# Attention layer with low-rank experts: the q, k and v projections made of split F32R operands

## The reference

```
qkv_in = rat_read(hidden, ...)          # three groups of 512 features per token:
    x = res.reshape(b, l, 512, 4)
    y = einsum('blhc,hoc->bloh', x, W)  # o = 0, 1, 2: q, k, v
    yn = (y - mean) * rsqrt(var + eps) * gamma + beta
q = einsum('bli,oi->blo', q_in, qkv_w[0])   # 512 x 512, the same for k and v
q, k = rope(q, pos), rope(k, pos)           # 16 heads of 32
scores = q k^T / sqrt(32), causal; o = softmax(scores) v
hidden = rat_write(hidden, o, ...)
... a second rat_read, a gated product with the context, a second rat_write,
    then low-rank experts
```

## Time and profile before

| what | us |
|---|---|
| median of 3 runs (lowest to highest) | 1682.9 (1682.56 to 1685.71) |
| the profiled execution's own time | 1683.9 |
| its span | 1682.1 |
| TensorE busy in the span | 1571.4 |
| VectorE busy | 1132.0 |
| ScalarE busy | 906.1 |
| GpSimd busy | 340.0 |
| projections (start to the first score) | 270.2 |

### The profile page before, as it was taken

One profiled execution on the slowest core, in us unless ns is written; L12 is line 12 of the kernel. 1 busy time (PEld: TensorE's weight loads), 2 busy tenths in 40 slices (PEclk: granted clock), 3 DMA queues, 4 the chain that ended last, 5 costly groups with the idle time before them and its releaser, 6 DMA issues.

```text
span 1682.1 us, 24567 instructions
## 1 busy us (share of the span) xinstructions
PE 1571.4 (93%) x9238; PEld 1170.6 (70%) x9238; DVE 1132.0 (67%) x1758; ACT 906.1 (54%) x1672; POOL 340.0 (20%) x326
## 2 busy tenths in 40 slices
PE   7999999999999987699999999898999999999986
PEld 6565555666666655577898777697777788875654
DVE  7877754888888867644463774874675864546777
ACT  5334235888888864445543566553567634543443
POOL 1424534555434300110002010012000002000000
PEclk8999999999999998699999999999999999999998
DMA  9657567999987646267677665567675666655642
GB/s 358 221 196 304 182 170 236 282 284 279 269 224 198 188 173 200 108 206 231 207 234 226 228 233 194 187 228 227 225 244 193 202 214 209 226 194 179 222 181 100
DMA packets 129370, 364.29 MB, mean 217 GB/s; under 512 B 15954, under 2 KB 45266, under 8 KB 113892
## 3 DMA queue, kind: packets, MB, share of 16 engines
q1 hardware_dynamic: 128964, 362.59, 66.9%
q10 hardware_dynamic: 288, 0.13, 0.0%
HBM read 276.55 MB, written 86.11 MB: 216 GB/s over the span
## 4 chain that ended last, share of the span: by engine, by line
PE 75%; DVE 13%; ACT 6%; issue 3%; DMA 2%; POOL 1%; SPq 0%; DVEq 0%; ACTq 0%
PE ps L1626 20%; PE ps L1638 8%; PE ps L555 7%; PE ps L1048 5%; PE ps L1035 4%; PE ps L1071 4%; PE ps L1651 4%; PE ps L1569 3%; PE ps L1541 3%; PE ps L1596 3%; PE ps L1584 3%; PE ps L514 3%; ACT a_p L1150 3%; PE ps L1526 3%; PE ps L1556 1%
## 5 line engine op out<-in xcount | busy, mean ns | idle before, releaser
L1626 PE MATMUL ps<-m_y_split,m_win 128*128 128x512 f32 x1536 | 388.5, 407 | 8.0 <-issue 7.8
L1626 PEld LDWEIGHTS ps<-m_y_split,m_win 128*128 128x128 f32 x1536 | 287.1, 191 | 78.3 <-issue 14.0
L1092 DVE TENSOR_REDUCE a_negmax<-ps 128x1 f32<-128x640 f32 (+7 forms) x176 | 180.8, 1027 | 59.8 <-PE ps L1038 58.8
L1150 ACT ACTIVATE a_p<-ps,a_negmax 128x128 f32<-128x128 f32 (+7 forms) x256 | 188.7, 750 | 28.9 <-DVE a_negmax L1092 26.6
L1638 PE MATMUL ps<-m_wods,m_y_split 128*128 128x316 f32 x768 | 179.2, 321 | 0.9 <-DVE m_hT L1823 0.9
L1048 PE MATMUL ps<-ident,a_p 128*128 128x128 f32 x1152 | 157.5, 275 | 1.3 <-DVE a_pT L1105 1.2
L1861 ACT ACTIVATE m_turned<-ps 128x512 f32<-128x512 f32 x128 | 74.7, 595 | 135.1 <-PE ps L1526 124.1
L1035 PE MATMUL ps<-a_k,a_q 128*128 128x512 f32 (+3 forms) x384 | 124.1, 402 | 16.0 <-ACT a_p L1150 14.1
L1638 PEld LDWEIGHTS ps<-m_wods,m_y_split 128*128 128x128 f32 x768 | 127.7, 191 | 3.8 <-issue 2.4
L1048 PEld LDWEIGHTS ps<-ident,a_p 128*128 128x128 f32 x1152 | 123.7, 142 | 3.4 <-DVE a_pT L1105 1.9
L1823 DVE TENSOR_TENSOR m_hT<-m_raw,ps 128x512 f32<-128x512 f32 x64 | 43.8, 685 | 112.7 <-PE ps L1626 112.2
(11 more groups left out here) (217 smaller groups left out, 2939.1 us busy)
## 6 DMA issues: line engine op xcount, KB each, us to landing
m_win<-mlp_in_split SPq DMA_DIRECT2D x128, 512.0 KB, 4.0
m_wods<-mlp_out_split SPq DMA_DIRECT2D x96, 316.0 KB, 3.2
m_wod<-in_wod1T SPq DMA_DIRECT2D x64, 316.0 KB, 2.9
p_xT<-in_xT SPq DMA_DIRECT2D x16, 1024.0 KB, 8.9
p_x<-in_x SPq DMA_DIRECT2D x16, 1024.0 KB, 10.4
a_q<-qk_split SPq DMA_DIRECT2D x64, 256.0 KB, 7.1
a_k<-qk_split SPq DMA_DIRECT2D x128, 128.0 KB, 7.0
mlp_in_split<-a_w_two SPq DMA_DIRECT2D x32, 512.0 KB, 5.4
```

The costliest lines, as they stand in the source:

```text
L1092: V.tensor_reduce(negmax[:, n % 4, 0:len(units[n][3])], by_head(n, score_banks(n)), AX_X, ALU.max, negate=True).then_inc(max_ready, 1)
L1150: m = S.activation(dst[:, j, :], src[:, j, :], ACT.Exp, bias=negmax[:, n % 4, j:j + 1], accum_out=rsum[:, si % 2, q * 4 + hh:q * 4 + hh + 1])
L1626: m = nc.tensor.matmul(bank_of("m", blk, step), win[s][:, wl, ic, :], y[k], start=(ic == 0 and p3 == 0), stop=(ic == HCH - 1 and p3 == 2))
```

## The change

Each operand of the q, k and v products is split into an upper half, rounded to F32R, and a lower half, the rest. Each product of two float32 operands becomes three F32R products: upper by upper, upper data by lower weights, lower data by upper weights.

- TensorE: `qkv` issues 12 F32R matmuls per step instead of 4 float32 ones. The turns of v (k = 8 to 11) leave the group before step 0 and stand between steps 3 and 4, after the read at step 3.
- ScalarE: `turn(blk, w)` makes the upper half of every k and the whole copy of those that VectorE doesn't (8 of 12); v's four come at step 3 ahead of `round_rope`. `weights_upper` makes the upper halves of the weights: q's before the first turn, k's after it, v's at step 3 of block 0.
- VectorE: `turn` makes whole copies of k = 0, 1, 4, 5, each after ScalarE's upper half, and lower halves of k = 0, 1; lower halves of q's weights ahead of, and of k's weights behind, the first block's turn.
- GpSimd: `lower` makes ten lower halves: k = 2 to 7 at the end of a block, 8 to 11 at step 3 behind the rotation and ahead of `read_a`; in block 0 also those of v's weights there.
- Buffers: y data in two sets of upper and lower halves of four k each (`halves_of`, `halves_are_free`); three rotation buffers in which the halves are made in place (`RR`), instead of two and four for halves; one table buffer and one `p_v` instead of two; five y buffers instead of six; the angles share the rotation buffers' place.
- SP: a block's table is loaded at the end of the block before; `load_first_heads` moves from after block 2 to step 3 of block 3, behind `store_qk` of pair 1.

```diff
-        XR, YR = 2, 6
+        XR, YR, RR = 2, 5, 3
...
-        wq = sb("p_wqkv", [P, 3 * HCH, H])
+        whi = sb("p_wqkv_hi", [P, 3 * HCH, H], F32R)
+        wraw = sb("p_wqkv", [P, 3 * HCH, H])
+        place[0] = wraw_place
+        wlo = sb("p_wqkv_lo", [P, 3 * HCH, H], F32R)
...
         def turn1_before(blk, k):
-            return 6 * blk + k // 4
+            return 6 * blk + (0, 1, 3)[k // HCH]
         def qk_before(blk, n):
-            return 6 * blk + 3 + n // 4
+            return 6 * blk + (2, 4)[n // 4]
+        RAW_BY_DVE, LO_BY_DVE = (0, 1, 4, 5), (0, 1)
+        def halves_of(blk, k):
+            s = (3 * blk + k // HCH) % 2
+            return yh[s][:, k % HCH, :], yl[s][:, k % HCH, :], yT[s][:, k % HCH, :]
+        def halves_are_free(e, blk, w):
+            if w == 1:
+                e.wait_ge(v_mm, 4 * blk)
+            else:
+                e.wait_ge(qk_mm, 8 * blk + 2 * w)
...
             def qkv(blk):
                 for n in range(8):
+                    if n == 4:
+                        turn(blk, 2)
                     pe.wait_ge(emptied[b], qk_before(blk, n))
+                    pe.wait_ge(whi_ready, HCH * w + HCH)
                     if w:
-                        pe.wait_ge(wkv_loaded, 16)
+                        pe.wait_ge(wklo_ready, HCH)
+                    else:
+                        pe.wait_ge(tables_ready, WQ)
                     for ic in range(HCH):
                         k = w * HCH + ic
-                        pe.wait_ge(emptied[4 + k % 4], turn1_before(blk, k) + 1)
-                        m = nc.tensor.matmul(ps[:, b, :], wq[:, k, col:col + P], yT[:, k, :],
-                                             start=(ic == 0), stop=(ic == HCH - 1))
+                        upper_is_there(blk, k)
+                        for j, ww in enumerate((whi, wlo)):
+                            nc.tensor.matmul(ps[:, b, :], ww[:, k, col:col + P], halves_of(blk, k)[0],
+                                             start=(ic == 0 and j == 0), stop=False)
+                    for ic in range(HCH):
+                        k = w * HCH + ic
+                        lower_is_there(blk, k)
+                        m = nc.tensor.matmul(ps[:, b, :], whi[:, k, col:col + P], halves_of(blk, k)[1],
+                                             start=False, stop=(ic == HCH - 1))
...
         # project_dve, turn(blk)
+                def raw(k):
+                    dve.wait_ge(turn1_mm, 12 * blk + k + 1)
+                    halves_are_free(dve, blk, k // HCH)
+                    dve.wait_ge(y1hi_ready, 12 * blk + k + 1)
+                    V.tensor_scalar(halves_of(blk, k)[2], ps[:, b, :], gam1[:, k:k + 1], bet1[:, k:k + 1],
                                     ALU.mult, ALU.add).then_inc(emptied[b], 1)
+                def lower(k):
+                    dve.wait_ge(emptied[b], turn1_before(blk, k) + 1)
+                    V.tensor_tensor(ylo_, whole, yhi_.bitcast(F32), ALU.subtract).then_inc(y1lo_dve, 1)
+                raw(0); raw(1); lower(0); lower(1); raw(4); raw(5)
             def rope(blk, pair):
-                dve.wait_ge(lo_ready, 2 * u - 2)
+                dve.wait_ge(split_stored[s], rope_stored_before(u, s))
...
         # project_dve, once
-            V.tensor_scalar(wq[:, 0:HCH, :], wq[:, 0:HCH, :], float(1.0 / np.float32(np.sqrt(HD))), None,
-                            ALU.mult).then_inc(tables_ready, 1)
+            for k in range(HCH):
+                dve.wait_ge(whi_ready, k + 1)
+                m = V.scalar_tensor_tensor(out=wlo[:, k, :], in0=wraw[:, k, :], scalar=QSCALE,
+                                           in1=whi[:, k, :].bitcast(F32), op0=ALU.mult, op1=ALU.subtract)
+            m.then_inc(tables_ready, 1)
             turn(0)
+            for k in range(HCH, 2 * HCH):
+                dve.wait_ge(whi_ready, k + 1)
+                V.tensor_tensor(wlo[:, k, :], wraw[:, k, :], whi[:, k, :].bitcast(F32),
+                                ALU.subtract).then_inc(wklo_ready, 1)
...
         # project_act
+            def weights_upper(w):
+                for k in range(HCH * w, HCH * w + HCH):
+                    act.wait_ge(wkv_loaded if w else wq_loaded, 16)
+                    S.activation(whi[:, k, :], wraw[:, k, :], ACT.Copy,
+                                 scale=1.0 if w else QSCALE).then_inc(whi_ready, 1)
+            def turn(blk, w):
+                for k in range(HCH * w, HCH * w + HCH):
+                    act.wait_ge(turn1_mm, 12 * blk + k + 1)
+                    halves_are_free(act, blk, w)
+                    S.activation(yhi_, ps[:, b, :], ACT.Identity, bias=bet1[:, k:k + 1],
+                                 scale=gam1[:, k:k + 1]).then_inc(y1hi_ready, 1)
+                    if k not in RAW_BY_DVE:
+                        S.activation(whole, ps[:, b, :], ACT.Identity, bias=bet1[:, k:k + 1],
+                                     scale=gam1[:, k:k + 1]).then_inc(emptied[b], 1)
...
-            turn(0)
+            weights_upper(0)
+            for w in range(2):
+                turn(0, w)
+            weights_upper(1)
             for blk in range(NBLK):
                 for step in range(12):
+                    if step == 3:
+                        turn(blk, 2)
+                        if blk == 0:
+                            weights_upper(2)
                     if step < 8 and step % 2:
                         round_rope(blk, step // 2)
...
         # project_pool
+            def lower(blk, ks):
+                for k in ks:
+                    pool.wait_ge(emptied[4 + k % 4], turn1_before(blk, k) + 1)
+                    pool.wait_ge(y1hi_ready, 12 * blk + k + 1)
+                    G.tensor_tensor(ylo_, whole, yhi_.bitcast(F32), ALU.subtract).then_inc(y1lo_pool, 1)
+            lower(0, range(2, 2 * HCH))
             for blk in range(NBLK):
                 for step in range(12):
                     if step < 8 and step % 2:
                         rope(blk, step // 2)
+                    if step == 3:
+                        lower(blk, range(2 * HCH, 3 * HCH))
+                        if blk == 0:
+                            for k in range(2 * HCH, 3 * HCH):
+                                pool.wait_ge(whi_ready, k + 1)
+                                G.tensor_tensor(wlo[:, k, :], wraw[:, k, :], whi[:, k, :].bitcast(F32),
+                                                ALU.subtract).then_inc(wvlo_ready, 1)
                     if blk + 1 < NBLK and step in READ_AT:
                         t, part = READ_AT[step]
                         (read_b if part else read_a)((blk + 1) * TB + t)
+                if blk + 1 < NBLK:
+                    lower(blk + 1, range(2, 2 * HCH))
...
         # project_sp
                     if step < 8 and step % 2:
                         store_qk(blk, step // 2)
+                    if blk == NBLK - 1 and step == 3:
+                        load_first_heads()
...
-                if blk + 2 < NBLK:
-                    load_tab(blk + 2)
-                if blk == NBLK - 2:
-                    load_first_heads()
+                if blk + 1 < NBLK:
+                    load_tab(blk + 1)
+                sp.wait_ge(emptied[7], v_before(blk) + 1)
+                move(v_d[b, :, t0 // P:t0 // P + TB, :], p_v[:, :, :]).then_inc(v_stored, 16)
```

More of the change, by code:

```diff
@@ L283, in program @@
         bet1 = sb("p_beta1", [P, RD1 * HCH])
-        tab = [sb(f"p_cos_sin{i}", [P, 2, BLK]) for i in range(2)]
-        yT = sb("p_yT", [P, RD1 * HCH, BLK])
-        rt = sb("p_rope", [P, 2, 4, BLK])
-        hi = sb("p_rope_hi", [P, 2, 2, BLK], F32R)
-        lo = sb("p_rope_lo", [P, 2, 2, BLK], F32R)
-        p_v = [sb(f"p_v{i}", [P, TB, H]) for i in range(2)]
+        tab = sb("p_cos_sin", [P, 2, BLK])
+        yh = [sb(f"p_yT_hi{i}", [P, HCH, BLK], F32R) for i in range(2)]
+        yT_place = place[0]
+        yT = [sb(f"p_yT{i}", [P, HCH, BLK]) for i in range(2)]
+        place[0] = yT_place
+        yl = [sb(f"p_yT_lo{i}", [P, HCH, BLK], F32R) for i in range(2)]
+        rt_place = place[0]
+        rt = sb("p_rope", [P, RR, 4, BLK])
+        rt_end, place[0] = place[0], rt_place
+        posi = sb("p_pos_i", [P, T // 8], I32)
+        ang = sb("p_angle", [P, T // 8])
+        kk = sb("p_turns", [P, T // 8])
+        sn = sb("p_sine", [P, 2, T // 8])
+        assert place[0] <= rt_end
+        place[0] = rt_end
+        p_v = sb("p_v", [P, TB, H])
         p_st = sb("p_stats", [P, 2, 4, 6])
@@ L309, in program @@
         ks = [sb(f"a_k{i}", [P, L], F32R) for i in range(NS)]
-        a_v = [sb(f"a_v{i}", [P, TPB, P]) for i in range(VR)]
+        a_v = [sb(f"a_v{i}", [P, TPB, P]) for i in range(VR - 1)]
         assert place[0] <= reads_end
+        a_v.append(sb(f"a_v{VR - 1}", [P, TPB, P]))
         a_p = [sb(f"a_p{i}", [P, L]) for i in range(PR)]
@@ L482, in turn1_before, with rope_stored_before @@
         def turn1_before(blk, k):
-            return 6 * blk + k // 4
```

(35 more changed lines are left out.)

103 lines of the change are left out of this document (57 added, 46 removed).

## The result

The changed kernel takes 1722.76 us in the median (1720.53 to 1725.23) against 1682.9 (1682.56 to 1685.71): ratio 1.0231, 95% interval 1.0211 to 1.025 (four executions of each; the recorded ratios are not the quotients of the medians, here and below). That is 2.8 us above the 1720 predicted. The profiled execution of after took 1720.71 us, its span is 1718.9; that of before 1683.9 and 1682.1. The two spans differ by 36.8 us, and all of it is there when attention's first scores of its second unit start: at 271.28 before, at 309.13 after, 37.85 later. Here is where it came from.

A forecast was written before the change was run, and what follows sets the result against it. TensorE was taken to bound the projections before, VectorE's chain with its `rstd` wait after. From 1683.9 us, +19.2, + 2 x 5.5 and + 0.9 gave +31, clock +6: 1721, so median 1720; range 1688 to 1733.

The forecast's parts named there:

- A: Likeliest case, projection blocks: VectorE waits for GpSimd's late `rstd` and blocks lengthen; median 1720 us, chance 0.70.
- The wait for `rstd`: VectorE at L637, with GpSimd's `rstd` queued behind lower halves: 7.3 us in blocks 1 and 2, 14 in block 0.
- The chain from T to T: VectorE's path between starts of ScalarE's evictions in successive blocks: 67.8 us against 62.34, 5.5 more; block 0 75.7.
- Weight halves in block 0: VectorE's lower halves of k's weights end at 11.9 us instead of 6.7; holds by GpSimd, up to 4.9, taken as 0.
- The edits put at nothing: Fewer table, `p_v`, y and rotation buffers: no cost; if a cover fails, 5 to 10 us once per block.
- TensorE: In the projections: F32R matmuls 0.236 us apart, and some 5 us idle between v's last product and the turns.
- The clock: TensorE at half rate after idle gaps, at three block ends and attention's start: 5 to 7 us, bounds 0 and 12.
- The last block: Attention's first scores wait for heads 0 to 3, loaded behind `store_qk(1)`: 46 us against 45.2, 0.8 to 1 lost.
- the 302 to 309: Sign that the forecast is right: attention's first score at about 302 to 309 us.
- The sum: Whole kernel: +19.2, + 2 x 5.5, + 0.9 = +31 us, clock +6: 1721 profiled, median 1720.
- B: Rival: the `rstd` wait costs little and VectorE's chain alone sets the block, 61.3 us; +5, 1688 us, chance 0.14.
- C: Rival: TensorE keeps setting the projections' pace, block 56.2 us; -14, 1669 us, chance 0.12.

The follow-up runs named there:

- The first experiments: Changed kernel with GpSimd's `rstd` moved ahead of v's lower halves, 1718.47 us, or ahead of the second pair's lower halves as well, 1723.67 us.
- the four with one edit: Changed kernel with `rstd` ahead of v's lower halves, 1718.47 us; of the pair's too, 1723.67; third product left out, 1716.8; heads' loads ahead of second pair's stores, 1719.38.
- both powers first: Changed kernel with GpSimd's `rstd` ahead of the second pair's lower halves and v's lower halves behind the second power, at step 4: 1712.51 us.
- the new shares alone: both powers first, plus ScalarE copying k = 4, 5 and GpSimd making all lower halves of q's and k's chunks and k's weights: 1702.96 us.
- f1: the new shares alone, plus TensorE's next-but-one block read ahead of the turns, its tile and the heads loaded earlier: 1683.31 us against 1684.77 before, ratio 0.9996.
- the version with four copies: f1 with VectorE also writing the whole copies of chunks 2 and 3: 1682.42 us against 1682.91 for the kernel before, ratio 0.9986.

## Why the prediction was right

The likeliest case (A) came true with its mechanism; the terms:

- **The wait for `rstd`.** Predicted 7.3 us in blocks 1 and 2; 6.66 and 6.67 measured. VectorE asks at T + 32.8 (predicted 32.75) and gets it at 39.5 (40.0): ScalarE rounds until T + 31.9 (31.95). In block 0 about 14 predicted, 13.67 measured. The size of each wait was right; its worth was not quite what the step says. The first experiments show that moving `rstd` alone gains 0.5 to 1.1 a block, since the second power, a few instructions behind it in VectorE's list, stands behind the same halves in GpSimd's. The prediction named one request of two.
- **The chain from T to T.** The first rotation ends at T + 16.5 (16.5), the second at 25.6 (25.6), the fourth at 49.0 (49.4), the last y copies start at 64.7 (65.2). Block 67.3 against 67.8. The 19.26 at the second T against 19.2 is two misses that cancel: block 0 lasted 76.5 against 75.7, and it began 1.5 us later than before, not 2.25.
- **Weight halves in block 0.** The lower halves of k's weights were costed with no hold by GpSimd. They took 4.63 us for four, held each time, and VectorE was free for the sums at T + 13.2 instead of 11.9:

```profile
45.57 1.28 DVE L739 TENSOR_TENSOR p_yT_lo<-p_yT,p_yT_hi 128x512 fp32r<-128x512 f32 x2
...
51.80 4.63 DVE L811 TENSOR_TENSOR p_wqkv_lo<-p_wqkv,p_wqkv_hi 128x512 fp32r<-128x512 f32 x4 [2.26 <-ACT p_wqkv_hi L865]
```

  Two such halves take 1.28 us where GpSimd had hardly begun (first row), and 2.32 for two in the second. The same in block 1: 2.36 for the two of L739. The rule on the two sides of SBUF (the Trainium skill, SBUF — State Buffer, "SBUF: two separate sides") that the prediction weighed and put at 0 is borne out, at about 2 of the 4.9 us that it allowed.
- **The edits put at nothing.** VectorE has no wait for a store or a table in blocks 0 to 2 of after, so buffers and tables cost nothing there.
- **TensorE.** It was idle for 5.0, 3.4 and 5.0 us ahead of the turns (5 predicted), and its matmuls start 0.234 us apart (0.236 predicted), as v's last ones show:

```profile
294.33 0.39 PE L630 MATMUL ps<-p_wqkv_hi,p_yT_lo 128*128 128x512 f32 x1
294.56 0.40 PE L630 MATMUL ps<-p_wqkv_hi,p_yT_hi 128*128 128x512 f32 x1
294.80 0.39 PE L630 MATMUL ps<-p_wqkv_lo,p_yT_hi 128*128 128x512 f32 x1
```

- **The clock, predicted 5 to 7 us, was nothing at the block ends.** The granted clock did fall there, as foreseen. Just behind the third gap:

```profile
252.00:254.00 2.00, 1.41 (x7) 1.41 (x8) 0.00 (x0) 2.00 (x4) 0.00 (x0) 0.50 0.01 4
```

  Sixteen turns took 3.68 us at 188.71, where it was 0.50, and 1.91 at 70.08. But these turns had begun 1.7 us ahead of T, the first product came at T + 5.8 at all three block ends, and from 258 on the clock was 1.00 again. Elsewhere the half rate fell in stretches in which nobody waited for TensorE: block 0 shows 0.83 and a read of 6.62 us at 63.62, and VectorE has no wait for a product there. Where the scores wait for their loads, the 128x256 scores take 0.56 us where they took 0.36, but the span behind S is no longer than before (1409.8 against 1410.8).
- **The last block is the term that was mis-sized.** The prediction gave 46 us from T to the scores, +0.9; it took 54.8, +8.6 (S against S). The very first score was at 295.96, since head 0 was in by then; the 302 to 309 foreseen for it came true for the last head, 308.77. `store_qk(1)` was issued until T + 27.2 as foreseen (27), the 25 issues took 15.2 us instead of 13.5, and the last load landed 12 us behind its issue, not 5 to 7. That price came from the page's median of 7 us over all loads of the kernel, and landing times grow along the row of loads. The k loads of heads 0 to 3 have medians of 4.1, 5.6, 8.4 and 9.8 us in before and of 5.1, 6.4, 10.6 and 11.5 in after. Of the last head, in before and in after:

```profile
DMA to landing us min/median/max: 9.7/9.8/10.0
```
```profile
DMA to landing us min/median/max: 11.3/11.5/12.2
```

  So three of the five us missed stood in the trace of before: its last loads took 10, not 7. For the other 2 us the two stretches of after:

```profile
280.00:300.00 20.00, 16.65 (x74) 13.20 (x72) 3.24 (x6) 4.59 (x8) 15.62 (x13) 0.96 0.95 207
300.00:316.00 16.00, 6.79 (x26) 4.84 (x27) 2.99 (x4) 5.02 (x21) 0.00 (x0) 0.50 0.83 239
```

  Full engines alone don't explain them: while the 25 loads were issued the DMA share was 0.96 in after and 0.96 in before. What goes with them is stores issued just ahead of the loads in the same queue. After and the six other kernels that have such stores (the four with one edit, both powers first, the new shares alone) show a longest landing of 12.0 to 13.3 us; before and f1, where no store stands just ahead, show 10.0 and 8.5. No run changed this alone, so it is not shown as the cause.
- **The sum.** +31 and +6 of clock were predicted, 37; measured 37.85 at S and 36.8 in the span. The clock's 6 and the last block's 7.7 stood in for one another, which is luck: with the clock at nothing and all else as predicted the forecast would have been 1714, 9 us under the result.
- **The rivals.** B's condition, VectorE reaching L704 without a wait, was made twice; its 61.3 us a block was too low, 66.3 with `rstd` alone (the second power waited) and 63.8 with both powers (GpSimd held VectorE's small instructions, 3.1 us a block). C decides nothing: removing 11.3 us of TensorE's work moved a block by 1.9.

## What to carry to other kernels

When work is moved to an idle engine, its busy time says little: look up each small request that a busier engine makes of it, all of them and not only the first, and see what now stands ahead in its queue. And see which of the busier engine's instructions will run beside it: two of them took 2 us of the 5.5 that a better order had gained. Here the order of four queues and the shares of the work cost 40 us, and the same products with other orders and shares nothing. Price a transfer by the rows of its own place in the queue, the last of its row if that is the one awaited, not by its median over the kernel.

## What the runs showed of the hardware

A VectorE instruction with two SBUF inputs can be held through several GpSimd instructions, not only one. In f1 this multiplication of two columns, 0.12 us elsewhere, took 4.93 while GpSimd went through four 128x512 instructions without a gap, and ended with the last of them:

```profile
91.87 4.93 DVE L706 TENSOR_TENSOR p_moments<-rstd 128x1 f32<-128x1 f32 x1 [1.24 <-POOL rstd L933]
```
```profile
91.27 0.56 POOL L933 TENSOR_TENSOR rstd<-p_moments,mhalf 128x1 f32<-128x1 f32 x1
91.79 1.30 POOL L953 TENSOR_TENSOR p_rope<-p_rope 128x512 f32<-128x512 f32 x1
93.03 1.30 POOL L954 TENSOR_TENSOR p_rope<-p_rope 128x512 f32<-128x512 f32 x1
94.28 2.50 POOL L959 TENSOR_TENSOR p_rope<-p_rope 128x512 fp32r<-128x512 f32 x2
```

VectorE lost the turn four times in a row. The timed execution of f1 and the version with four copies show the same 4.93 us at this place. And it isn't only instructions with two tensors: the scaling of 128x3 values by a column (L707 above, in the kernel with `rstd` ahead of the pair) took 1.35 us beside GpSimd's halves, 0.23 beside none.
